# Order of VectorE's and ScalarE's work in groups two and three of a split-precision conditional residual kernel

## The reference

```
attn = tanh(x @ W1 + b1);  s = attn @ v                      # one score per row
p    = softmax(where(mask[type], s, -1e30)) / count(mask)    # 128 x 128, mask: prefix, postfix or all but itself
z    = x + p @ x
out  = z + z @ W[cat] + b[cat]                               # W: 64 categories x 512 x 512
```

## Time and profile before

| | before |
|---|---|
| median of 3 runs | 309.99 us (309.94 to 310.02) |
| profiled execution: its time | 309.99 us |
| its span | 308.2 us |
| TensorE (PE) busy | 300.3 us, 97% |
| VectorE (DVE) busy | 278.4 us, 90% |
| ScalarE (ACT) busy | 262.5 us, 85% |
| GpSimd (POOL) busy | 86.9 us, 28% |
| moved by DMA | 105.69 MB, mean 343 GB/s |

### The profile page before, as it was taken

The page is one execution under the profiler, slowest core; times in us unless marked ns, Lnnn a source line. Parts: engine busy times, 40 slices in busy tenths (PEclk is TensorE's granted clock), DMA queues, the critical chain, the costliest instruction groups (busy, mean ns, idle before and its releaser), DMA issues.

```text
span 308.2 us, 4890 instructions
## 1 busy us (share of the span) xinstructions
PE 300.3 (97%) x1284; PEld 232.8 (76%) x1284; DVE 278.4 (90%) x385; ACT 262.5 (85%) x429; POOL 86.9 (28%) x119
## 2 busy tenths in 40 slices
PE   7999999799999999999999999999999999999995
PEld 4445587688887878878787887878888787887884
DVE  4447799999999999999999999999999999999961
ACT  2263988989999998999999899999989999899942
POOL 5020402334152233414214341422434132302100
PEclk9999999999999999999999999999999999999999
DMA  7999999999999999999998999999999999986133
GB/s 261 408 388 415 395 412 381 422 358 291 376 371 332 407 335 407 350 369 357 343 392 303 412 361 368 370 318 398 305 405 361 352 391 349 397 303 222 61 136 136
DMA packets 23516, 105.69 MB, mean 343 GB/s; under 512 B 2625, under 2 KB 2626, under 8 KB 13378
## 3 DMA queue, kind: packets, MB, share of 16 engines
q1 hardware_dynamic: 23058, 103.03, 89.2%
q10 hardware_dynamic: 432, 2.36, 2.0%
HBM read 88.61 MB, written 16.78 MB: 342 GB/s over the span
## 4 chain that ended last, share of the span: by engine, by line
PE 83%; issue 10%; DMA 2%; POOLq 1%; ACT 1%; DVE 1%; POOL 0%; ACTq 0%
PE ps_y L679 16%; PE ps_y L681 16%; PE ps_y L680 16%; PE ps_pre L638 12%; PE ps_y L691 4%; PE ps_y L692 4%; PE ps_y L693 4%; PE ps_y L697 3%; DMA w_raw<-in_L_cond_W 2%; PE ps_pT L655 2%; POOLq L290 1%; PE ps_y L667 1%; PE ps_scores L648 1%; PE ps_scores L646 1%; ACT probs L363 0%
## 5 line engine op out<-in xcount | busy, mean ns | idle before, releaser
L481 DVE TENSOR_TENSOR w_lo<-w_raw,w_hi 128x2048 fp32r<-128x2048 f32 x58 | 135.1, 2329 | 0.5 <-ACT w_hi L348 0.5
L348 ACT ACTIVATE w_hi<-w_raw 128x2048 fp32r<-128x2048 f32 x58 | 111.8, 1928 | 8.1 <-POOL w_raw L284 7.5
L679 PE MATMUL ps_y<-w_hi,xT_hi 128*128 128x512 f32 x232 | 91.7, 395 | 0.0
L681 PE MATMUL ps_y<-w_hi,xT_lo 128*128 128x512 f32 x232 | 90.5, 390 | 0.0
L680 PE MATMUL ps_y<-w_lo,xT_hi 128*128 128x512 f32 x232 | 90.3, 389 | 0.0
L284 POOL TENSOR_TENSOR w_raw<-w_raw,ident 128x512 f32<-128x512 f32 x26 | 33.6, 1294 | 113.1 <-DVE w_lo L481 74.7
L681 PEld LDWEIGHTS ps_y<-w_hi,xT_lo 128*128 128x128 f32 x232 | 43.5, 188 | 9.4
L509 DVE TENSOR_TENSOR z_lo<-ps_y,z_hi 128x512 fp32r<-128x512 f32 x64 | 43.6, 683 | 7.7 <-ACT z_hi L384 7.7
L680 PEld LDWEIGHTS ps_y<-w_lo,xT_hi 128*128 128x128 f32 x232 | 43.6, 188 | 8.8
L384 ACT ACTIVATE z_hi<-ps_y 128x512 fp32r<-128x512 f32 x64 | 38.9, 609 | 13.2 <-PE ps_y L681 5.1
L679 PEld LDWEIGHTS ps_y<-w_hi,xT_hi 128*128 128x128 f32 x232 | 43.6, 188 | 8.7
(11 more groups left out here) (70 smaller groups left out, 363.0 us busy)
## 6 DMA issues: line engine op xcount, KB each, us to landing
w_raw<-in_L_cond_W SPq DMA_DIRECT2D x62, 1024.0 KB, 8.2
out<-out_sb SPq DMA_DIRECT2D x64, 256.0 KB, 6.1
x_raw<-in_x SPq DMA_DIRECT2D x15, 1024.0 KB, 7.1
out_sb<-in_L_cond_b SPq DMA_DIRECT2D x16, 256.0 KB, 5.4
w_raw<-in_L_cond_W ACTq DMA_DIRECT2D x2, 1024.0 KB, 7.2
x_raw<-in_x SPq DMA_DIRECT2D x2, 512.0 KB, 4.9
w_pack<-in_W_b_v ACTq DMA_DIRECT2D x1, 257.0 KB, 2.9
b_raw<-in_L_cond_b SPq DMA_DIRECT2D x2, 128.0 KB, 8.9
```

Of the source, the lines that this page charges most:

```text
L348: nc.scalar.activation(w_hi[k % NH][:], w_raw[k % NW][:], ACT.Copy).then_inc(w_hi_ready, 1)
L481: nc.vector.tensor_tensor(w_lo[k % NL][:], w_raw[k % NW][:], w_hi[k % NH][:].bitcast(F32), ALU.subtract).then_inc(w_lo_ready, 1)
L679: nc.tensor.matmul(y[:], xT_hi[q][:, c, xs], w_hi[k % NH][:, c, :], start=(c == 0), stop=False)
L681: last = nc.tensor.matmul(y[:], xT_lo[q][:, c, xs], w_hi[k % NH][:, c, :], start=False, stop=(c == DC - 1))
```

## The change

Only the order of calls changes. No instruction is added or removed, and the loops are as before.

```diff
 (ScalarE)
             tanh_group(1)
-            split_z_hi(3)
             split_xT_hi(2)
             exp_group(1)
+            split_w_hi(6)
             copy_out(0)
+            split_z_hi(3)
+            split_w_hi(7)
+            split_z_hi(4)
             scale_group(1)
-            split_z_hi(4)
-            split_w_hi(6)
-            copy_out(2)
+            split_w_hi(8)
             split_z_hi(5)
             split_mix_hi(1)
-            split_w_hi(7)
-            copy_out(3)
+            copy_out(2)
             tanh_group(2)
-            split_w_hi(8)
             split_w_hi(9)
             split_z_hi(6)
+            copy_out(3)
+            split_w_hi(10)
+            exp_group(2)
             copy_out(4)
-            exp_group(2)
-            split_w_hi(10)
 (VectorE)
             max_group(1)
-            split_z_lo(3)
             add_identity(6)
+            split_xT_lo(2)
             row_scale_group(1)
-            split_xT_lo(2)
             add_wide(0)
             add_identity(7)
-            split_z_lo(4)
             split_w_lo(6)
-            split_mix_lo(1)
+            split_z_lo(3)
             add_identity(8)
             split_w_lo(7)
+            split_z_lo(4)
+            split_w_lo(8)
+            add_identity(9)
+            split_mix_lo(1)
+            split_av_lo(2)
             split_z_lo(5)
-            split_av_lo(2)
-            add_identity(9)
-            split_w_lo(8)
             add_identity(10)
             max_group(2)
             split_w_lo(9)
-            row_scale_group(2)
             split_z_lo(6)
             add_identity(11)
+            row_scale_group(2)
```

## The result

| | before | changed |
|---|---|---|
| median (runs) | 309.94 us (7) | 308.33 us (7) |
| lowest to highest | 309.73 to 310.02 | 307.69 to 309.07 |
| profiled execution: time, span | 309.99, 308.2 | 308.65, 306.9 |
| ratio to before, 95% interval | | 0.9931 (0.9908 to 0.9954) |

The changed kernel is faster. The medians differ by 1.6 us; the ratio, which compares executions of both kernels, times 309.94 gives 307.8 us (307.1 to 308.5). Between lowest and highest run lie 1.4 us, against 0.3 before; it is not shown that the change brings this, since the kernel before spread over 1.6 to 3.1 us in the four later sets of runs.

What follows compares the result with a forecast made beforehand. TensorE, 97% busy, was taken as the bound, with 2.57 us of stalls ahead of hidden(3). hidden(3) at 58.07 - 0.68 + 1.0 = 58.4, started at 58.45, gained 1.5 us: 309.99 - 1.5 = 308.5 us, range 307.9 to 309.5.

Steps and rivals of the forecast that it cites:

- the sum: hidden(3) at 58.45 instead of 59.96, 1.5 us gained; 309.99 - 1.5 = 308.5 us.
- the new stall at pz(3): TensorE's pz(3), before at 37.61, waits for z_lo(3) until 38.6: 1.0 us lost.
- the 47.4 for max_group(2): VectorE reaches max_group(2) at 47.4 us, when the scores are there.
- The bound and the two stalls: TensorE, 97% busy, bounds; stalls at pz(6), 0.68 us, and hidden(3), 1.89 us, total 2.57; VectorE's 1.87 us idle can be filled.
- ScalarE and VectorE of group two: Third x first: xT_hi(2) at 28.95, xT_lo(2) at 31.94, row_scale(1) 34.35, z_lo(3) 37.85.
- GpSimd held: GpSimd's row_div, asked for at 32.3, is held until VectorE's xT_lo(2) ends: done at 34.32; alone it took 0.20 us.
- the stall at pz(6): TensorE's 0.68 us loss at pz(6) disappears, since z_lo(6) runs at 50.6 and is wanted at 53.3.
- The bias row: Bias row 1, issued about 48.9 instead of 47.16, keeps its queue place and lands at 54.66: cost nothing.
- the distance of 1.5 us from store 3 to the row: In the DMA queue: store 3 landed at 53.2, bias row 1 at 54.7; taken as the queue's spacing, not the issues'.
- The end: Behind hidden(3) TensorE is the bound, each engine 1.5 us early; VectorE's slack of about 0.25 us per group stays.

Runs made afterwards that it cites:

- e2: Kernel before with only the third x ahead: xT_hi(2) before z_hi(3) on ScalarE, xT_lo(2) before row_scale(1) on VectorE; 310.07 us, ratio 1.0016.
- e3: Changed kernel with third x, z(3) and row_scale(1) back in the old order, W splits, z and copies behind them as changed; 309.50 us, ratio 0.9984.
- e8: Changed kernel with one VectorE swap, row_scale(1) ahead of xT_lo(2) again; 308.28 us, ratio 0.9955.
- e11_after_look: Changed kernel run and profiled again, no edit; median 308.42 us, profiled execution 307.97 us.
- e1b_after: Changed kernel run and profiled again, no edit; median 308.53 us, profiled execution 309.11 us.
- e4: Changed kernel with the load of x of group 3 behind that of W 10 in SyncE's queue; 309.89 us, ratio 0.9994.
- e9: Changed kernel with copy_out(3) right behind copy_out(2) on ScalarE, so store(3) and bias row 1 are issued sooner; one execution, 308.21 us.
- e6: Changed kernel reordered to remove the stall at pz(3), with z(3), copy_out(0), scale_group(1) and mix_lo(1) earlier; 309.34 us, ratio 0.9969.
- e10: Changed kernel with x of group 3 loaded earlier, no pz(3) stall, and xT_lo(3) ahead of add_wide(1) and add_identity(12); 309.19 us, ratio 0.998.

## Why the prediction was nearly right, and where it was not

The mechanism came out as forecast and the median, 308.33, lies 0.2 us from the forecast of 308.5; by the ratio the time is 307.8, 0.7 us from it and just under the range. The step that failed is a size: the 1.0 us that the sum charges for the new stall at pz(3), and with it the 47.4 for max_group(2). The runs show 0.66 us and 46.99.

- **The bound and the two stalls: right.** VectorE's idle time ahead of 34 us was filled except for the 1.34 us for W 6, pz(6) waits no more and hidden(3) starts sooner. That both halves are needed (e2, e3) the prediction didn't say.
- **ScalarE and VectorE of group two: right**, where 0.14 us of each difference is the early execution: xT_hi(2) at 28.63 (28.95 forecast), row_scale(1) 34.11 (34.35), z_lo(3) 37.68 (37.85).
- **GpSimd held: right.** row_div ended at 34.08, with xT_lo(2) (34.02); e8 shows it short where nothing holds it. The section "SBUF: two separate sides" of the "SBUF — State Buffer" page of the Trainium skill, which I drew on, agrees with both traces (2.06 against 0.20 us).
- **The new stall at pz(3): the term that was mis-sized.** I charged TensorE 1.0 us. pz(3) did come 0.94 us late (38.41, against 37.61 less the 0.14), but the transposes only 0.66 (39.45, against 38.93 less the 0.14). Straight behind xw_raw(5), pz(3)'s first matmul held the next back 0.63 us (37.61 to 38.24 before); behind a stall 0.34 (38.41 to 38.75). The wait swallowed 0.29 us of that switch. In the same way the stall at pz(6) was worth 0.78 us and not 0.68: from transposes to transposes TensorE needed 18.79 us before (38.93 to 57.72) and 18.01 in the changed kernel (39.45 to 57.46). Scores sooner by 0.3 us make max_group(2) sooner: 46.99 in e11_after_look, 47.4 forecast, with 0.1 for the early execution. From there VectorE's list took the forecast 8.6 us: xT_lo(3) starts at 55.62 and hidden(3) at 58.01, where the forecast had 56.0 and 58.45. That execution took 307.97 us. So where W 10 is in time the execution ends 0.5 us below my sum, 0.14 of it by the early start, and a low end of 307.9, only 0.6 below the sum, left too little room. The runs down to 307.44 are faster still; what they have besides is not known.
- **W 10: the step that is missing.** I had add_identity(10) at 46.5 and W 10 landed at 46.3 before: 0.2 us of margin, never named. In the first profile VectorE waited 0.84 us, and hidden(3) came 0.70 later than in e11_after_look (58.71, 58.01); in e1b_after it waited 1.3. The two errors have opposite signs, and the median of 308.33 lies 0.2 us from the forecast partly for that reason: that is luck.
- **The bias row: right that it costs nothing; its landing was met by luck.** It was issued at 48.61 (48.9 forecast) and landed at 54.7 as before. But the distance of 1.5 us from store 3 to the row, which I took for the queue's, was 0.6 here (54.1 to 54.7), while the queue ahead was 0.9 us later; the two cancel. With the same issue the row landed at 53.4 in e11_after_look and at 55.5 in e1b_after. e4 shows a row that is waited for.
- **The end: right.** Behind hidden(3) nothing is won or lost in the changed kernel's executions.

## What to carry to other kernels

When a list is moved forward by a microsecond or two, write beside each of its steps when its inputs land, the DMA ones too: a margin that was 2 us becomes the new wait. A DMA queue with a backlog gives each transfer a place, not a latency: a late issue costs nothing while the queue is full (the bias row in e9), and a gap left in it delays everything behind (e4: 2.7 us at the bias row). That has a limit: W 13, issued at 50.53 instead of 48.53, landed 3.5 us behind the row in the changed kernel (58.2) and 2.4 before (57.1), 1.1 us later; there the queue did run short, and only because nobody waited for W 13 did it cost nothing. If the late engine's list is solid, further reordering only chooses where the other engine stalls (e6, e10).

## What was not expected of the hardware

The same 1 MB transfer, W 9, issued at the same time (33.9 to 34.0 us) with the same transfers ahead of it (W 8 landed at 36.9 to 37.2), took 5.9, 7.0 and 7.8 us in three executions of one kernel, and what stood behind it in the queue, W 10 too, came late with it. And the first matmul of split operands straight behind plain f32 ones holds the next back 0.63 us, against 0.34 us after a pause; a stall at that point is 0.29 us cheaper than it looks. The traces show this (0.63 at three such places of the kernel before: 27.76, 33.26 and 37.61) but not the reason.
